# Mixture-of-experts layers on Trainium2: four tiles ahead of a loop of six instead of two

## The reference

```python
scores = sigmoid(x @ gate_w)                       # 2048 x 32 experts
selected_experts = top_k(masked_scores, 6)         # 6 experts for each token
x_exp = repeat(x, 6, axis=0); sort_idx = argsort(selected_experts.ravel())
xs = x_exp[sort_idx]                               # 12288 rows, sorted by expert
group_sizes = bincount(selected_experts.ravel(), 32)
g = ragged_dot(xs, w_gate, group_sizes)            # 512 -> 352
u = ragged_dot(xs, w_up, group_sizes)              # 512 -> 352
d = ragged_dot(silu(g) * u, w_down, group_sizes)   # 352 -> 512
out = sum of the 6 rows of each token, weighted    # + a shared expert
```

## Time and profile before

| what | value |
|---|---|
| median of 3 runs | 3204.13 us (3201.19 to 3208.88) |
| the profiled execution: time, span | 3201.4 us, 3199.3 us |
| granted TensorE clock, mean over the span | 0.977 |
| first experts stage, first to last L1840 | 1103.5 to 1875.7 us, 116 tiles |
| second experts stage, first to last L1840 | 2419.9 to 3189.6 us, 116 tiles |
| TensorE matmul busy | 3047.5 us (95%) |

### The profile page before, as it was taken

How to read it: one execution, slowest core, us unless ns; L and a number is a source line. 1 busy time by engine, 2 the same in 40 slices (tenths; PEclk the granted TensorE clock), 3 DMA queues, 4 the chain that set the end, 5 groups by cost and what they waited for, 6 DMA issues and landing times. The chain is left out here.

```text
span 3199.3 us, 62766 instructions
## 1 busy us (share of the span) xinstructions
PE 3047.5 (95%) x15680; PEld 2409.0 (75%) x15683; DVE 2073.4 (65%) x3875; ACT 1591.1 (50%) x2094; POOL 866.7 (27%) x777
## 2 busy tenths in 40 slices
PE   8979999999899999999999969988999999999998
PEld 6845555554688799999999954436878999999997
DVE  5266666663686566666666659997765666666665
ACT  3224444544321366666656657734125566666664
POOL 0021100010011233333343323341123343343333
PEclk9969999999999999999999989999999999999999
DMA  5331111130311476766776650114026777776664
GB/s 191 112 80 42 41 41 40 41 85 23 126 30 37 123 188 165 178 171 165 172 180 172 137 149 13 39 54 146 24 69 179 184 185 179 176 175 173 170 151 77
DMA packets 140488, 374.52 MB, mean 117 GB/s; under 512 B 21984, under 2 KB 24800, under 8 KB 136800
## 3 DMA queue, kind: packets, MB, share of 16 engines
q1 hardware_dynamic: 86624, 244.01, 24.2%
q0 software_dynamic: 52608, 127.69, 20.8%
q10 hardware_dynamic: 1152, 1.57, 0.2%
HBM read 275.39 MB, written 97.81 MB: 117 GB/s over the span
## 5 line engine op out<-in xcount | busy, mean ns | idle before, releaser
L1884 DVE TENSOR_TENSOR first_lo<-first_raw,first_hi x230 | 557.8, 2425 | 108.0 <-ACT first_hi L1829 107.5
L1829 ACT ACTIVATE first_hi<-first_raw x230 | 465.9, 2025 | 31.9 <-DMA first_raw<-in_expert_weights_dram 14.6
L607 ACT ACTIVATE b_probs<-b_p_cols 128x1024 f32<-128x1024 f32 (+1 forms) x320 | 269.3, 893 | 298.5 <-PE b_p_cols L739 297.4
L1877 DVE TENSOR_TENSOR g_hidden<-g_gate,g_p_up 128x352 f32<-128x352 f32 x232 | 120.9, 521 | 446.3 <-PE g_p_up L1944 443.9
L1840 ACT ACTIVATE g_y<-g_p_y,first_rows_in 128x512 f32<-128x512 f32 x232 | 159.8, 689 | 340.5 <-PE g_p_y L1960 339.7
L1942 PE MATMUL g_p_gate<-first_hi,first_rows_hi 128*128 (+1 forms) x928 | 319.4, 344 | 4.4 <-DVEq L1900 4.4
L638 DVE TENSOR_REDUCE b_part_max<-b_p_ring 128x1 f32<-128x512 f32 x384 | 246.4, 686 | 117.3 <-PE b_p_ring L724 115.0
L1781 POOL DMA_INDIRECT mixed_rows<-g_y,first_ids_out x116 | 186.3, 1606 | 446.4 <-ACT g_y L1840 351.9
L1781 POOL DMA_INDIRECT out_dram<-g_y,first_ids_out x116 | 186.8, 1610 | 443.9 <-ACT g_y L1840 338.5
L1943 PE MATMUL g_p_gate<-first_lo,first_rows_hi 128*128 (+1 forms) x928 | 301.1, 325 | 0.0
L1944 PE MATMUL g_p_gate<-first_hi,first_rows_lo 128*128 (+1 forms) x928 | 299.9, 323 | 0.0
(11 more groups left out here) (369 smaller groups left out, 6453.4 us busy)
## 6 DMA issues: line engine op xcount, KB each, us to landing
first_raw<-in_expert_weights_dram SPq DMA_DIRECT2D x248, 544.0 KB, 8.0
qk_hi<-a_hi SPq DMA_DIRECT2D x32, 256.0 KB, 2.6
qk_lo<-a_lo SPq DMA_DIRECT2D x32, 256.0 KB, 3.0
xn_rows<-f_xn SPq DMA_DIRECT2D x8, 1024.0 KB, 8.5
b_q_stack<-qk_hi SPq DMA_DIRECT2D x28, 256.0 KB
b_k_stack<-qk_hi SPq DMA_DIRECT2D x28, 256.0 KB
first_raw<-in_expert_weights_dram SPq DMA_DIRECT2D x2, 2176.0 KB, 8.5
resid<-in_x_dram SPq DMA_DIRECT2D x4, 1024.0 KB, 10.8
```

The source lines that it names most:

```text
L607: act.activation(probs[:, q, :, 0:w], p_cols[:, m % NCOL, :, 0:w], ACT.Exp, scale=SCALE).then_inc(probs_ready, 1)
L1829: act.activation(hi[:, bass.ds(place, PIECE)], raw[:, bass.ds(source, PIECE)], ACT.Copy).then_inc(split_hi_ready, 1)
L1884: v.tensor_tensor(lo[:, bass.ds(place, PIECE)], raw[:, bass.ds(source, PIECE)], hi[:, bass.ds(place, PIECE)].bitcast(F32), ALU.subtract).t ...
```

## The change

BASE = 4 tiles are written out ahead of the loop instead of 2, so that a stage runs 4 + 6n tiles where it ran 2 + 6n. n_turns becomes `(end[31] + 6 - 1 - 4) // 6`, the least n with 4 + 6n >= end[31]. MAX_TURNS is 25 as before (148 / 6, rounded up), and so is the loop's body, apart from the numbers of slots and semaphore counts, which are moved along by two tiles.

```diff
+BASE = 4
-MAX_TURNS = -(-(MAX_TILES - 2) // PER_TURN)
+MAX_TURNS = -(-(MAX_TILES - BASE) // PER_TURN)
-COLUMNS = 2 + MAX_TURNS * PER_TURN + AHEAD + 1
+COLUMNS = BASE + MAX_TURNS * PER_TURN + AHEAD + 1
...
-                            chain.link(v.tensor_scalar(disp.n_turns[:], end[0:1, E - 1:E], PER_TURN - 3.0, 171.0, ALU.add, ALU.mult))
+                            chain.link(v.tensor_scalar(disp.n_turns[:], end[0:1, E - 1:E], PER_TURN - 1.0 - BASE, 171.0, ALU.add, ALU.mult))
...
         def in_turn(r, q):
-            return r * PER_TURN + 2 + q
+            return r * PER_TURN + BASE + q
...
# GpSimd
                 add(0, 0, 0)
+                for t in range(2, BASE):
+                    add(t - 1, (t - 1) % NROWS, (t - 1) % NY)
+                    pool.wait_ge(turned, t - 1)
+                    pool.sem_inc(gather_order, 1)
+                    gather(t + AHEAD, (t + AHEAD) % NROWS)
                 with pool.Fori(0, MAX_TURNS) as r:
...
-                add(n_turns * PER_TURN + 1, 1, 1)
+                add(n_turns * PER_TURN + BASE - 1, (BASE - 1) % NROWS, (BASE - 1) % NY)
...
# ScalarE
                 split_next(1, *piece)
+                for t in range(2, BASE):
+                    piece = next_piece(t)
+                    silu(t, t % 2)
+                    split_next(t, *piece)
+                    scale_y(t - 1, 1 - t % 2, (t - 1) % NY, (t - 1) % NROWS)
+                    copy_hidden(t, t % 2)
+                    copy_rows(t + 2, t % 2)
                 with act.Fori(0, MAX_TURNS) as r:
...
# VectorE
                 rest_of_piece(1, *piece)
+                for t in range(2, BASE):
+                    piece = next_piece(t)
+                    multiply(t, t % 2)
+                    rest_of_piece(t, *piece)
+                    rest_of_hidden(t, t % 2)
+                    rest_of_rows(t + 2, t % 2)
+                    next_ids(t, (t + AHEAD) % NROWS, t % NROWS)
                 with v.Fori(0, MAX_TURNS) as r:
...
# TensorE
                 turn_rows(3, 1, None)
+                before, here = 0, where(2)
+                for t in range(2, BASE):
+                    up(t, t % 2, here)
+                    after = where(t + 1) if t < BASE - 1 else None
+                    down(t - 1, 1 - t % 2, before)
+                    before, here = here, after
+                    turn_hidden(t, t % 2)
+                    pe.wait_ge(rows_lo_ready, t + 2)
+                    turn_rows((t + 2) % NROWS, t % 2, 1)
                 with pe.Fori(0, MAX_TURNS) as r:
...
-                down(n_turns * PER_TURN + 1, 1, last_at)
+                down(n_turns * PER_TURN + BASE - 1, (BASE - 1) % 2, last_at)
```

More of the change, by code:

```diff
@@ L1795, in _ @@
                             t = in_turn(r, q)
-                            add(t - 1, (1 + q) % NROWS, (1 + q) % NY)
+                            add(t - 1, (BASE - 1 + q) % NROWS, (BASE - 1 + q) % NY)
                             pool.wait_ge(turned, t - 1)
                             pool.sem_inc(gather_order, 1)
-                            gather(t + AHEAD, (2 + q + AHEAD) % NROWS)
-                add(n_turns * PER_TURN + 1, 1, 1)
+                            gather(t + AHEAD, (BASE + q + AHEAD) % NROWS)
+                add(n_turns * PER_TURN + BASE - 1, (BASE - 1) % NROWS, (BASE - 1) % NY)
                 for i in range(NROWS):
-                    pool.wait_ge(gathered[i], (n_turns + 1 if i >= AHEAD else n_turns) * 16)
+                    pool.wait_ge(gathered[i], (n_turns + len(range(i, BASE + AHEAD, NROWS)) - (i < AHEAD)) * 16)
                     pool.sem_inc(gather_order, 1)
-                pool.wait_ge(added, (n_turns * PER_TURN + 2) * 16)
+                pool.wait_ge(added, (n_turns * PER_TURN + BASE) * 16)
                 pool.sem_inc(add_order, 1)
@@ L1825, in split_next @@
                     act.sem_inc(hi_free, 1)
-                    if not isinstance(t, int):
+                    if not (isinstance(t, int) and t < 2):
                         act.wait_ge(tiles_done, t - 1)
@@ L1862, in _ @@
                             split_next(t, *piece)
-                            scale_y(t - 1, 1 - i, (1 + q) % NY, (1 + q) % NROWS)
+                            scale_y(t - 1, 1 - i, (BASE - 1 + q) % NY, (BASE - 1 + q) % NROWS)
                             copy_hidden(t, i)
                             copy_rows(t + 2, i)
-                scale_y(n_turns * PER_TURN + 1, 1, 1, 1)
+                scale_y(n_turns * PER_TURN + BASE - 1, (BASE - 1) % 2, (BASE - 1) % NY, (BASE - 1) % NROWS)
             @block.vector
@@ L1924, in _ @@
                             rest_of_rows(t + 2, i)
-                            next_ids(t, (2 + q + AHEAD) % NROWS, (2 + q) % NROWS)
+                            next_ids(t, (BASE + q + AHEAD) % NROWS, (BASE + q) % NROWS)
             @block.tensor
@@ L1936, in up @@
                 def up(t, i, at):
-                    pe.wait_ge(split_done, 2 if isinstance(t, int) else t + 2)
+                    pe.wait_ge(split_done, 2 if isinstance(t, int) and t < 2 else t + 2)
                     pe.wait_ge(rows_lo_ready, t + 1)
@@ L1969, in _ @@
                 n_turns = turns(pe)
-                last_at = where(n_turns * PER_TURN + 1)
+                last_at = where(n_turns * PER_TURN + BASE - 1)
                 turn_hidden(0, 0)
@@ L1989, in _ @@
                             pe.wait_ge(rows_lo_ready, t + 2)
-                            turn_rows((4 + q) % NROWS, i, r + 1)
-                down(n_turns * PER_TURN + 1, 1, last_at)
+                            turn_rows((BASE + 2 + q) % NROWS, i, r + (BASE + 2 + q) // NROWS + (1 if (BASE + 2 + q) % NROWS >= AHEAD else 0))
+                down(n_turns * PER_TURN + BASE - 1, (BASE - 1) % 2, last_at)
 NEG = -1e38
```

## The result

The changed kernel took 3193.59 us in the median of 5 runs (3189.43 to 3195.3), the kernel before 3204.13 us in the median of 5 (3201.19 to 3208.88). The ratio is 0.9956, with a 95% interval of 0.9942 to 0.997. The two medians lie 10.5 us apart; the ratio stands for 14.1 us, its interval for 9.6 to 18.6 us. Forecast were 3190 us, in a range of 3184 to 3197, and faster. A second set of 11 runs gave a smaller gain, 0.9973 (0.9962 to 0.9984), which is 8.7 us (5.1 to 12.2); it is told with the experiments. Each set has its own runs of the kernel before, and a ratio is always against those of its set.

The account below looks back on a forecast made before the run. TensorE's row of tiles was taken to bound both experts stages. +13.4 - 26.7 + 0.7 = -12.6 us gave 3188.8 us from the profiled execution and 3191.5 from the median; forecast 3190 us, range 3184 to 3197.

Parts of the forecast that it names:

- The bound: Both experts stages: each is as long as TensorE's row of tiles, at 6.68 us a tile.
- The number of tiles: Experts stages: end[31] is 115 in the first and 112 in the second, giving 118 and 112 tiles, for 116 each.
- one tile of work more in the second layer: Rival, second stage: end[31] is 113, so both stages have 118 tiles, +26.7 us, 3228 us; chance 2%.
- The sum: Both experts stages: +13.4 us for two tiles more, -26.7 for four fewer, +0.7 for a jumped turn, -12.6 us.
- The jumped turn: Second stage's loop end: seven turns jumped instead of six, exposed on TensorE's sequencer, +0.74 us; first stage +0.
- Written-out code: Tiles 2 and 3, now ahead of the loop: taken as 0, saving at most 0.3 us a stage or costing 3.6 us.
- No fetch in the loop: Experts loops: every engine's body stays loaded; the rival, a fetch at every turn, had 3229 us and chance 3%.
- The Trainium skill's rule on taken branches: Experts loops: a taken branch outside the present two 16 KiB pages forces a fetch; the prediction said it fails for TensorE.
- the late weights: Experts stages: the one late weight load goes away or doubles, 4.1 us either way, 3186 or 3194 us; no chance given.

Follow-up runs that it names:

- the kernel with nineteen turns: The changed kernel with loops that count to 19 instead of 25 on all engines; ratio 0.9959, median 3194.0 us.

## Why the prediction held, point by point

**The bound.** TensorE's row of tiles sets the stage's length: shown by the steps of 6.68 us in every kernel and by 112, 116 and 118 tiles taking 747, 770 and 783 us.

**The number of tiles.** 115 and 112 tiles with work, read from the reference's routing and confirmed by when two weight loads were issued, gave 118 and 112, and so the trace has it. This was the step on which all hung: without it, the forecast could only have said between -52 and +27 us. The kernel with 118 tiles in both layers shows what one tile of work more in the second layer would have cost, 3235.53 us.

**The sum.** +13.4 us for the first stage: in the means over the table's profiles 783.9 against 771.2 us, +12.7; without the late steps 782.3 and 769.0, +13.3. Second stage, -26.7 + 0.7 = -26.0: 747.1 against 769.0 us, -21.9; without the late steps 743.7 and 768.9, -25.2. What remains of the difference to -26.0 is in the last step, which in the four profiles of the kernel before lies between -0.8 and +0.8 us, as the clock behind the pause is full or half. The forecast did not have this effect of the clock. The sum of both stages without lateness is -11.9, forecast were -12.6.

**The jumped turn** cost 0.75 us and is exposed in full, as costed (0.74); TensorE's wait is 3.6 us, where 3.5 were forecast. The Trainium skill's figure (Advanced Engine Details and Errata, Control Flow Timing), 108 ns for a compare-and-branch, is half of the 218 ns that six of the seven in the rows above take; the one that leaves the loop takes 86.

**Written-out code** at 0: six more tiles of it made 1.0008, with 0 inside the interval, and the first steps of a stage have the same length with two, four and eight tiles written out (8.4 and 5.8 us). What that kernel's second stage had in addition, 8.9 us of late steps, is not in those tiles: the longest is at 2674 us, in the loop.

**No fetch in the loop.** Between 1160 and 1880 us all queues that moved anything in the changed kernel were these two; one packet of instructions falls just ahead, at 1150 to 1160 us, in the loop's first turns.

```profile
q0 software_dynamic: 24162, 58.28, 42.8%
q1 hardware_dynamic: 15557, 60.18, 25.5%
```

The Trainium skill's rule on taken branches (Runtime: NRT & Kernel Launch, Instruction fetch mechanics) did not come into force here either. For TensorE the prediction read it too strictly: the same section gives that engine 128 KiB, and a turn of 662 records in the trace at 64 bytes, some 42 KB by estimate, fits into that. What the trace contradicts is only the two pages of 16 KiB.

**What the sum did not have** is where the late weights fall. The forecast kept them out of the sum and in the range, as 4.1 us either way. In the two profiles that it compares, the lateness of both stages together went from 4.1 to 3.7 us, so it cost nothing, but it moved from the first stage to the second; in the means over the table's profiles it went from 2.3 to 5.0 us, which is inside that term. Of the 3.6 us between the forecast of 3190 us and the median of 3193.59 no single cause is shown: the profiled execution lies 4.8 us above the 3188.8 of the sum, and nearly all of that is outside the stages, 544.2 us between them in the one profile known then and 548.1 in this one. Whether the change gains less than the 12.6 us forecast is not settled either: the first set has 12.6 inside its interval (9.6 to 18.6 us), the second just outside (5.1 to 12.2 us).

**What stays open** is whether the lateness of the second stage belongs to the change. For it: none of four profiles of the kernel before had more than 0.3 us of it, all three of the changed kernel had more, and so had the kernels with 118 tiles in both layers (3.8 us), with two weight parts in flight (2.1 us) and, most of all, with eight tiles written out (8.9 us). Against it: the kernels with four tiles written out in the second layer and two in the first had 0.1, 0.2 and 0.1 us, the first of them with the changed kernel's own code in its second stage, and the kernel with nineteen turns had 0.7. What sorts all fourteen profiles is the first layer: with two tiles written out there the second stage was 0.0 to 0.3 us late in all seven, with four or eight 0.7 to 8.9 us in all seven. This order was seen only afterwards and no run was made to test it. It is not the number of tiles that the first stage runs, since the kernel with eight ran 116. The weak place is in both kernels: at the 18th or the 21st step of the second stage each profile of the kernel before is 0.4 to 1.1 us late and makes it up at the next step, and there the changed kernel's first two profiles are 4.0 and 4.4 us late. What in the written-out tiles of the first layer could move the weight loads of the second, no run isolates.

## What to carry to other kernels

Where a loop's count is rounded up, count first: find the real number of units in the data, confirm it by an event of the trace whose time depends on it, and multiply the difference by the measured cost of a unit. A padding unit costs what a working one costs, so a start that fits one layer can be wrong for the next; choosing it for each layer gave 0.991 where one choice for both gave 0.9956 and 0.9973. Before a few microseconds between two profiles are explained, take a second profile of the kernel before: here its first was 4 us short in a stretch in which the change only makes the tables two columns longer. And before a sum that fits is taken for a mechanism that fits, compare its parts: here two misses of 3 us cancelled.

## What the runs showed of the hardware

A jumped turn of a loop, with a test and a counter, costs 0.74 us on TensorE's sequencer, which 6 turns make 4.4 us of which 1.8 us were exposed. Its compare-and-branch takes 218 ns where it jumps and 86 ns where it falls through. A pause of TensorE of 2.8 to 3.6 us can cost more than itself, and its length alone doesn't tell: at the second stage's end half clock followed 2.83 us in the kernel before and the 3.6 us in the changed kernel, while 2.78 us in the former's second profile and the 2.88 us at 2564 us in the changed kernel were followed by matmuls 0.23 us apart, which is full clock.
